# A fused stack of four cross-attention layers: norm weights loaded first, first clears and masks moved to other engines, and the low part of a query taken before its bf16 copy

## Chip, cores and metric

One core of a Trainium2 chip. The metric is the device time in microseconds, the median of several executions. Engines are called by their names: TensorE (PE), VectorE (DVE), ScalarE (ACT), GpSimd (POOL) and SyncE (SP), which issues most of the DMAs.

## The reference

Four cross-attention layers run one after the other on x (4 batches, 1024 tokens, 256 channels) with one context (154 keys of 512 values for each batch). Layers 0 and 2 are "wide": 16 heads of 64, with a suppression of four chosen keys by two token masks. Layers 1 and 3 are "narrow": an RMS norm of x, then 16 query heads of 16 on 4 key heads. All is float32.

```python
# wide layer
logits = einsum('bhqd,bhkd->bhqk', x @ Wq, ctx @ Wk) * 64 ** -0.5
logits[..., token_indices_A] += -20 * (1 - mask_A)      # and B
out = softmax(logits) @ (ctx @ Wv)
x = x + out @ Wo + bo
# narrow layer
xn = x * rsqrt(mean(x * x) + 1e-5) * norm_w
x = x + softmax(einsum(xn @ wq, ctx @ wk) / 4) @ (ctx @ wv) @ wo
```

## The kernel before

**Prepare (about the first 190 us).** `prepare` transposes the context and the tokens, and splits each of the 20 pieces of weights (10 for each pair of a wide and a narrow layer) into a high and a low part: SyncE loads a piece into one of four buffers (`load_piece`, L332), ScalarE copies it to a float32r high part (L420), GpSimd subtracts to get the low part (L448). TensorE makes keys and values from the pieces, VectorE takes the products out of PSUM (L295 to L311), SyncE stores them to DRAM (`store_job`, L198) from four output buffers. The piece "nq" (the narrow layer's query weights) is first multiplied by the norm weights, on ScalarE (L414). The norm weights have one small tile for both pairs, so the load for the second pair (L340) waits until ten high parts are made, and each load is issued right behind the piece nq.

**Layers.** A window is one batch of one pair, 8 windows in all. A window has 16 steps n of 4 heads each, 8 wide and 8 narrow; the order of all work is written out by hand in the strings FIRST, ORDER and LAST, and every engine walks through the same list and does its own share of each entry. Entries that matter here:

- "query n k": TensorE multiplies the tokens by the query weights into one of three PSUM banks (L1528). ScalarE copies it as the high part into `q_pair` (L1279, L1280). VectorE then does four instructions: two casts of the high part to bf16 into `q_aux` (L1438, L1439), after which it signals `dve_aux`, and two subtractions of the high part from the product in PSUM into `q_pair` (L1440, L1441), after which it signals `dve_query`. There are 160 such entries.
- "max n k": TensorE makes bf16 logits from `q_aux` and the bf16 keys (wide L1545, narrow L1549), into the next of the three banks; the first for a query waits for `dve_aux`. VectorE reduces them to a maximum for each row (L1451). There are 1024.
- "turn n": the maxima are transposed (L1558) and written back as rows of `q_aux` by ScalarE (L1304).
- "rest n", "score n k", "value n k": the exact logits (bf16 rows and low parts, L1587, plus float32r, L1588), the exponentials (ScalarE L1292), the products with the values.
- "scale", "norm", "low", "output": GpSimd multiplies by the inverse sums (L1402), ScalarE and VectorE split the result (L1341, L1464), TensorE multiplies by the output weights (L1649), VectorE adds to x (L1484).

A bank of the three is used in turn by query, max, turn, output, square, rate and give; TensorE waits before each use until the reader of the use three before is done, and the reader of a query's bank is `dve_query`.

**The start of the layers.** VectorE clears five tiles (L1427: `w_top`, the first half of `q_aux`, `w_aux`, `w_aux_rest`, `tops`); SyncE waits for them by count and loads keys, key rows (`load_top_rows`, L1002), mask rows (`load_masks`, L1109) and the rest. GpSimd makes the identity, clears the second half of `q_aux` and other tiles, waits for all of VectorE's clears, and fills rows.

```python
nc.vector.tensor_copy(q_aux[0:64, t, s, j, :], q_pair[0:64, s, j, :])                    # L1438
nc.vector.tensor_copy(q_aux[64:P, ...], q_pair[64:P, ...]).then_inc(dve_aux.sem, 1)      # L1439
nc.vector.tensor_tensor(q_pair[64:P, s, j, :], ps[0:64], q_pair[0:64, ...], ALU.subtract)
last = nc.vector.tensor_tensor(...)                                                      # L1441
last.then_inc(dve_query.sem, 1)
```

Of the kernel before, what the change touches and what calls it, by code (L numbers as in the profile page):

```python
# [22 lines left out]
P = 128  # L23
# [56 lines left out]
def prepare(nc, ins, dr):  # L80

    ctx = ExitStack()
    with ctx:  # L83
# [17 lines left out]
        normw = sb("p_normw", [P, KC])  # L101
# [229 lines left out]
        def _(sp):  # L331
            def load_piece(i):  # L332
                if i >= SETS:
                    sp.wait_ge(s_lo, i - SETS + 1)
                p, name, src, st = pieces[i]
                sp.dma_start(view(raw, i), src).then_inc(s_w[i % SETS], 16)
                if name == "nq":
                    if p:
                        sp.wait_ge(s_hi, len(pieces) // 2)
                    sp.dma_start(normw[:, :], ins[f"L{2 * p + 1}_xattn_norm_w"].rearrange("(k p) -> p k", p=P)).then_inc(s_nw, 16)  # L340

            with nc.allow_non_contiguous_dma(reason="columns of norm weights"):
# [11 lines left out]
                load_piece(1)  # L354
                for i in range(2, SETS):
                    load_piece(i)
# [49 lines left out]
        def _(act):  # L406

            for i, (p, name, src, st) in enumerate(pieces):
                act.wait_ge(s_w[i % SETS], 16 * (i // SETS + 1))
                wait_piece_free(act, i)  # L410
                if name == "nq":
                    act.wait_ge(s_nw, 16 * (p + 1))
                    for k in range(KC):
                        nc.scalar.activation(view(raw, i)[:, k], view(raw, i)[:, k], ACT.Copy,  # L414
                                             scale=normw[:, k:k + 1]).then_inc(s_evh, 1)
                    act.wait_ge(s_evh, KC * (p + 1))
# [451 lines left out]
def layers(nc, ins, dr, out):  # L868

    ctx = ExitStack()  # L870
    with ctx:
# [45 lines left out]
        ROWS_CLEARED, NARROW_ROWS_CLEARED, CLEARED = 5, 3, 10  # L917
# [8 lines left out]
        rows_cleared = sem("rows_cleared")  # L926
# [56 lines left out]

        def bank_of(use):
            return general[:, USE[use] % GB, :]
# [3 lines left out]
        def _(sp):  # L989
# [3 lines left out]

            def rows_of(buf, par):

                a = 64 * (1 - par)
                return buf[a:a + 6].rearrange("p (h two) k -> p h two k", two=2)[:, :, par, :]

            def load_top_rows(p):

                for par in range(2):
                    sp.dma_start(rows_of(w_top, par), dr["keyrows"][p][:, None, :].to_broadcast([6, 8, KEYS])).then_inc(top_rows_loaded, 16)  # L1002
# [101 lines left out]

            def load_masks(t):

                for par in range(2):
                    a = 64 * (1 - par)
                    sp.dma_start(q_aux[a:a + 6, t].rearrange("p s (j two) n -> p (s j) two n", two=2)[:, :, par, :],  # L1109
                                 dr["maskrows"][t][:, None, :].to_broadcast([6, 4, TOK])).then_inc(masks_loaded[t], 16)  # L1110
# [26 lines left out]
            def each_entry():  # L1137

                for w, what, c, k in PLAN:
# [84 lines left out]
                    elif what == "wkeys" and w > 0:  # L1224

                        if k == 0:
                            wait(sp, pe_value.sem, pe_value.after(w - 1, "value", 11, 1))
                            if w == B:
                                load_top_rows(1)
# [5 lines left out]
            load_top_rows(0)  # L1235
            sp.wait_ge(rows_cleared, 2)
            load_masks(0)
            sp.wait_ge(rows_cleared, 4)
# [4 lines left out]
            load_masks(1)  # L1243
# [10 lines left out]
        def _(act):  # L1254
            def do(it, what, n, k):
# [37 lines left out]
                elif what == "turn":  # L1293

                    if (it, n) == (0, 0):
                        act.wait_ge(rows_cleared, 2)
# [51 lines left out]
        def _(pool):  # L1348
            nc.gpsimd.memset(ident[:], 0.0).then_inc(ident_ready, 1)
# [75 lines left out]
        def _(dve):  # L1425
            for buf in (w_top[:], q_aux[:, 0], w_aux[:], w_aux_rest[:], tops[:]):
# [3 lines left out]
            def do(it, what, n, k):  # L1430
                if what == "query":
# [3 lines left out]
                    t, s, j = half_of(n), slot(n), 2 * k  # L1435
                    if (it, n, k) == (0, 8, 0):
                        dve.wait_ge(cleared, 1)
                    nc.vector.tensor_copy(q_aux[0:64, t, s, j, :], q_pair[0:64, s, j, :])  # L1438
                    nc.vector.tensor_copy(q_aux[64:P, t, s, j + 1, :], q_pair[64:P, s, j + 1, :]).then_inc(dve_aux.sem, 1)  # L1439
                    nc.vector.tensor_tensor(q_pair[64:P, s, j, :], ps[0:64], q_pair[0:64, s, j, :], ALU.subtract)  # L1440
                    last = nc.vector.tensor_tensor(q_pair[0:64, s, j + 1, :], ps[64:P], q_pair[64:P, s, j + 1, :], ALU.subtract)  # L1441
                    last.then_inc(dve_query.sem, 1)
                elif what == "max":
# [283 lines left out]
```

## Time and profile before

| | us |
|---|---|
| median of 3 runs | 1754.18 (1751.69 to 1755.21) |
| the profiled execution | 1748.67 |
| its span, first to last instruction | 1746.9 |
| TensorE matmuls busy | 1617.9 (93%) |
| TensorE weight loads busy | 882.6 (51%) |
| VectorE busy | 1197.9 (69%) |
| ScalarE busy | 1023.9 (59%) |
| GpSimd busy | 471.9 (27%) |

How to read the profile's rows: times are microseconds from the start of the span. A row of the timeline has the start, how long it took, the engine, the line, the operation, what was written from what, its shape, how many were merged, and in brackets how long the engine had been idle before it and whose end released it. SPq rows are DMA issues in SyncE's queue. A row of groups has the busy time and the mean in ns, then the idle time before them. Ends of matmuls are modelled, and spans on GpSimd are rough.

### The profile page before, as it was taken

The numbers are of one execution on the slowest core, as the hardware profiler recorded it, in microseconds if no ns is written. First come the engines' busy times: TensorE is split into PE (matmuls) and PEld (weight loads), VectorE is DVE, ScalarE is ACT, GpSimd is POOL, SyncE is SP. The second block draws the span as 40 slices with busy tenths as digits, with TensorE's granted clock in tenths as the row PEclk, the third lists the DMA queues.
The fourth block names the chain that finished last, engine by engine and source line by source line (L and its number), as shares of the span: only waits on it lengthen the run. The fifth ranks groups of instructions, "written<-read, shape, count | busy, mean of one in ns | idle before, by whom it ended". The sixth has DMA issues, their size and how long they took to land.

```text
span 1746.9 us, 29686 instructions
## 1 busy us (share of the span) xinstructions
PE 1617.9 (93%) x10732; PEld 882.6 (51%) x10732; DVE 1197.9 (69%) x2313; ACT 1023.9 (59%) x1737; POOL 471.9 (27%) x353
## 2 busy tenths in 40 slices
PE   7998698999999999999999999899999999999794
PEld 6886444444545454544545454445454545454442
DVE  5474547676777687768777777678777877775551
ACT  2111165666667676767666766576676767676452
POOL 5342402123222231223131313132322322232212
PEclk9898898999999999999999999999999999999986
DMA  7998402151315121512353323412151325131422
GB/s 255 323 317 242 140 25 58 37 98 28 84 32 132 27 78 27 131 35 80 69 115 91 73 54 80 91 40 72 41 122 27 82 41 125 26 81 23 123 69 81
DMA packets 176738, 160.57 MB, mean 92 GB/s; under 512 B 91722, under 2 KB 133066, under 8 KB 175570
## 3 DMA queue, kind: packets, MB, share of 16 engines
q1 hardware_dynamic: 174578, 150.29, 33.5%
q10 hardware_dynamic: 2016, 8.39, 1.2%
q8 instruction: 87, 1.43, 0.3%
q14 instruction: 57, 0.47, 0.1%
HBM read 115.11 MB, written 43.48 MB: 91 GB/s over the span
## 4 chain that ended last, share of the span: by engine, by line
PE 46%; issue 16%; DVE 10%; POOL 7%; ACT 3%; SPq 3%; DMA 3%; POOLq 0%; ACTq 0%; DVEq 0%
PE general L1649 9%; PE general L1528 7%; POOL kept L1402 4%; PE score_ps L1587 4%; PE score_ps L1588 4%; PE out_ps L1605 4%; PE general L1545 3%; PE general L1549 3%; PE score_ps L1576 2%; PE out_ps L1625 2%; DVE q_pair L1440 2%; DVE q_aux L1439 2%; SPq L1135 2%; DVE q_pair L1441 2%; PE general L1669 2%
## 5 line engine op out<-in xcount | busy, mean ns | idle before, releaser
L1451 DVE TENSOR_REDUCE tops<-general 128x2 bf16<-128x308 f32 x1024 | 433.2, 470 | 88.1 <-PE general L1545 40.1
L1292 ACT ACTIVATE probs<-score_ps 128x512 f32<-128x512 f32 x512 | 297.7, 598 | 141.0 <-PE score_ps L1588 128.0
L1402 POOL TENSOR_TENSOR kept<-kept,inv_b 128x512 f32<-128x512 f32 x128 | 170.7, 1355 | 464.9 <-DMA inv_b<-scratch_inverses 464.9
L1438 DVE CAST q_aux<-q_pair 64x512 bf16<-64x512 f32 x160 | 74.8, 468 | 194.1 <-ACT q_pair L1280 192.9
L1304 ACT ACTIVATE q_aux<-general 4x512 bf16<-4x512 bf16 x320 | 187.5, 586 | 31.7 <-PE general L1558 26.1
L1279 ACT ACTIVATE q_pair<-general 64x512 fp32r<-64x512 f32 x160 | 94.6, 591 | 156.7 <-PE general L1528 156.1
L1545 PE MATMUL general<-w_top,q_aux 128*128 128x154 bf16 x1024 | 133.4, 237 | 36.5 <-DVE q_pair L1441 26.1
L1341 ACT ACTIVATE a_hi<-kept 128x512 fp32r<-128x512 f32 x160 | 93.6, 624 | 112.0 <-POOL kept L1402 48.1
L1464 DVE TENSOR_TENSOR a_lo<-kept,a_hi 128x512 fp32r<-128x512 f32 x160 | 123.9, 807 | 49.7 <-ACT a_hi L1341 48.9
L1392 POOL TENSOR_TENSOR x_lo<-xn,x_hi 128x1024 fp32r<-128x1024 f32 x31 | 73.6, 2375 | 285.0 <-ACT x_hi L1260 145.6
L1588 PE MATMUL score_ps<-q_pair,w_pair 128*128 128x512 f32 x256 | 149.4, 589 | 0.0
L1588 PE MATMUL score_ps<-q_pair,n_pair 128*128 128x512 f32 x256 | 147.0, 586 | 0.0
L1484 DVE TENSOR_TENSOR x<-general,x 128x512 f32<-128x512 f32 x160 | 106.7, 689 | 57.3 <-PE general L1649 56.2
L1545 PEld LDWEIGHTS general<-w_top,q_aux 128*128 128x128 bf16 x1024 | 63.0, 98 | 161.1 <-issue 98.4
L1549 PE MATMUL general<-n_top,q_aux 128*128 128x308 bf16 x512 | 129.2, 306 | 13.4 <-DVE q_pair L1441 8.9
L1316 ACT ACTIVATE kept<-out_ps 128x512 f32<-128x512 f32 x192 | 104.3, 595 | 61.6 <-PE sum_ps L1619 47.7
L1605 PE MATMUL out_ps<-probs,w_val 128*64 128x512 f32 x512 | 135.7, 615 | 0.0
L1402 POOL TENSOR_TENSOR kept<-kept,inv_n 128x512 f32<-128x512 f32 x64 | 83.1, 1320 | 179.4 <-DMA inv_n<-scratch_inverses 179.4
L1649 PE MATMUL general<-a_hi,wo_hi 128*128 128x512 f32 x256 | 107.8, 421 | 9.1 <-DVE a_lo L1464 3.6
L1549 PEld LDWEIGHTS general<-n_top,q_aux 128*128 128x128 bf16 x512 | 40.7, 97 | 146.2 <-issue 66.7
L1528 PE MATMUL general<-x_hi,wq_hi 128*128 128x512 f32 x256 | 110.0, 430 | 4.1 <-PEq L83 3.6
L1440 DVE TENSOR_TENSOR q_pair<-general,q_pair 64x512 fp32r<-64x512 f32 x160 | 109.5, 684 | 5.0
(157 smaller groups left out, 3305.7 us busy)
## 6 DMA issues: line engine op xcount, KB each, us to landing
inv_b<-scratch_inverses SPq DMA_DIRECT2D x128, 256.0 KB, 4.8
w_pair<-scratch_wk_hi SPq DMA_DIRECT2D x32, 256.0 KB, 4.9
x<-scratch_stream SPq DMA_DIRECT2D x16, 512.0 KB, 3.3
inv_n<-scratch_inverses SPq DMA_DIRECT2D x256, 32.0 KB, 1.9
xn<-scratch_stream SPq DMA_DIRECT2D x15, 512.0 KB, 3.4
scratch_stream<-x SPq DMA_DIRECT2D x14, 512.0 KB, 4.9
scratch_wk_hi<-p_kout_hi SPq DMA_DIRECT2D x16, 308.0 KB
p_raw<-in_L_xattn_Wk_dram SPq DMA_DIRECT2D x4, 1024.0 KB, 7.8
```

Source lines behind the costliest of these rows:

```text
L1292: nc.scalar.activation(dst, score_ps[:, number % 2, :], ACT.Exp, scale=scale).then_inc(act_exp.sem, 1)
L1304: last = nc.scalar.activation(q_aux[a:a + 4, half_of(n), slot(n), j, :], ps[0:4].bitcast(BF16)[:, 0:TOK], ACT.Copy, scale=-1.0)
L1402: last = nc.gpsimd.tensor_tensor(tiles[i], tiles[i], (inv_b, inv_n)[n % 2][:, i, :], ALU.mult)
L1440: nc.vector.tensor_tensor(q_pair[64:P, s, j, :], ps[0:64], q_pair[0:64, s, j, :], ALU.subtract)
L1451: last = nc.vector.tensor_reduce(tops[:, n % 2, sub, 2 * pair:2 * pair + 2], src, AX_X, ALU.max)
L1464: last = nc.vector.tensor_tensor(a_lo[:, i, :], kept[:, place(tile), :], a_hi[:, i, :], ALU.subtract)
L1528: last = nc.tensor.matmul(ps, l, r, start=(i == 0), stop=(i == len(pairs) - 1))
L1545: last = nc.tensor.matmul(ps[:, i * KEYS:(i + 1) * KEYS], q[:, 2 * pair + i, sub], w_top[:, 4 * (n % 4) + 2 * pair + i, :], start=True, st ...
L1549: last = nc.tensor.matmul(ps[:, 0:2 * KEYS], q[:, n % 2, sub], n_top[:, h:h + 2, :].rearrange("p h k -> p (h k)"), start=True, stop=True)
L1588: last = nc.tensor.matmul(ps, keys[0], q_pair[:, s, unit, :], start=False, stop=True)
L1605: last = nc.tensor.matmul(out_ps[64 * i:64 * i + 64, k, :], w_val[:, h * DW:(h + 1) * DW], probs[:, 2 * k + i, :], start=True, stop=False, ...
L1649: last = nc.tensor.matmul(ps, l, r, start=(i == 0), stop=(i == len(pairs) - 1))
```

## The change

The norm weights get a tile with a column pair for each pair of layers; both loads are issued by SyncE between the second and the third piece, with no wait, and ScalarE waits for both. The clear of the first half of `q_aux` moves from VectorE to the head of GpSimd's list, with a semaphore of its own. The first load of the key rows and of the mask rows (four DMAs) is issued by ScalarE ahead of its first copy; SyncE's waits are adapted. In each query step VectorE does the two subtractions first and the two casts after them.

```diff
-        normw = sb("p_normw", [P, KC])
+        normw = sb("p_normw", [P, 2, KC])
...
-                if name == "nq":
-                    if p:
-                        sp.wait_ge(s_hi, len(pieces) // 2)
-                    sp.dma_start(normw[:, :], ins[f"L{2 * p + 1}_xattn_norm_w"].rearrange("(k p) -> p k", p=P)).then_inc(s_nw, 16)
...
                 load_piece(1)
+                for p in range(2):
+                    sp.dma_start(normw[:, p, :], ins[f"L{2 * p + 1}_xattn_norm_w"].rearrange("(k p) -> p k", p=P)).then_inc(s_nw, 16)
                 for i in range(2, SETS):
...
-                    act.wait_ge(s_nw, 16 * (p + 1))
+                    act.wait_ge(s_nw, 16 * 2)
...
-        ROWS_CLEARED, NARROW_ROWS_CLEARED, CLEARED = 5, 3, 10
+        ROWS_CLEARED, NARROW_ROWS_CLEARED, CLEARED = 4, 3, 10
...
             sp.wait_ge(rows_cleared, 1)
             load_wide_keys(0, 0, 0)
-            load_top_rows(0)
-            sp.wait_ge(rows_cleared, 2)
-            load_masks(0)
-            sp.wait_ge(rows_cleared, 4)
+            sp.wait_ge(rows_cleared, 3)
             load_aux_rows(0)
...
         @block.scalar
         def _(act):
+            act.wait_ge(rows_cleared, 1)
+            load_top_rows(act, 0)
+            act.wait_ge(first_cleared, 1)
+            load_masks(act, 0)
...
                     if (it, n) == (0, 0):
-                        act.wait_ge(rows_cleared, 2)
+                        act.wait_ge(first_cleared, 1)
...
         @block.gpsimd
         def _(pool):
+            nc.gpsimd.memset(q_aux[:, 0].bitcast(F32), 0.0).then_inc(first_cleared, 1)
             nc.gpsimd.memset(ident[:], 0.0).then_inc(ident_ready, 1)
...
-            for buf in (w_top[:], q_aux[:, 0], w_aux[:], w_aux_rest[:], tops[:]):
+            for buf in (w_top[:], w_aux[:], w_aux_rest[:], tops[:]):
...
+                    if (it, n, k) == (0, 0, 0):
+                        dve.wait_ge(first_cleared, 1)
                     if (it, n, k) == (0, 8, 0):
                         dve.wait_ge(cleared, 1)
-                    nc.vector.tensor_copy(q_aux[0:64, t, s, j, :], q_pair[0:64, s, j, :])
-                    nc.vector.tensor_copy(q_aux[64:P, t, s, j + 1, :], q_pair[64:P, s, j + 1, :]).then_inc(dve_aux.sem, 1)
                     nc.vector.tensor_tensor(q_pair[64:P, s, j, :], ps[0:64], q_pair[0:64, s, j, :], ALU.subtract)
                     last = nc.vector.tensor_tensor(q_pair[0:64, s, j + 1, :], ps[64:P], q_pair[64:P, s, j + 1, :], ALU.subtract)
                     last.then_inc(dve_query.sem, 1)
+                    nc.vector.tensor_copy(q_aux[0:64, t, s, j, :], q_pair[0:64, s, j, :])
+                    nc.vector.tensor_copy(q_aux[64:P, t, s, j + 1, :], q_pair[64:P, s, j + 1, :]).then_inc(dve_aux.sem, 1)
```

`load_top_rows` and `load_masks` take the issuing engine as an argument and are otherwise as before.

## Rows read from the trace of the kernel before

**Rows 1.** Stages: us, busy time of each engine, granted clock, DMA share, GB/s

```profile
400.00:1600.00 1200.00, 1159.89 (x8047) 590.08 (x8045) 901.85 (x1721) 809.50 (x1394) 320.96 (x225) 1.00 0.29 69
```

**Rows 2.** Waits of TensorE: us in total, times, longest

```profile
PE general L1545 <- DVE q_pair L1441: 26.1, 26, 3.4
...
PE general L1549 <- DVE q_pair L1441: 8.9, 9, 2.0
```

**Rows 3.** Timeline, the prepare stage, its start and its end

```profile
16.66 1.91 ACT L420 ACTIVATE p_hi<-p_raw 128x2048 fp32r<-128x2048 f32 x1 [0.86 <-DMA p_raw<-in_L_xattn_Wk_dram]
...
20.83 4.62 POOL L448 TENSOR_TENSOR p_lo<-p_raw,p_hi 128x2048 fp32r<-128x2048 f32 x1
...
152.38 0.46 SPq L340 DMA_DIRECT2D p_normw<-in_L_xattn_norm_w_dram  x1
...
157.10 2.85 SPq L215 DMA_DIRECT2D scratch_wv<-p_vout  x4
...
164.99 0.69 DVE L304 COPY p_vout<-p_ps 104x512 f32<-104x512 f32 x1 [6.31 <-DMA scratch_wv<-p_vout]
```

**Rows 4.** Timeline, the start of the layers

```profile
194.42 0.59 ACT L1279 ACTIVATE q_pair<-general 64x512 fp32r<-64x512 f32 x1 [29.41 <-PE general L1528]
...
194.52 1.76 DVE L1427 MEMSET q_aux<- 128x2048 f32 x1 [0.37 <-issue]
...
196.80 0.86 SPq L1002 DMA_DIRECT2D w_top<-scratch_keyrows  x2
...
197.71 0.65 SPq L1109 DMA_DIRECT2D q_aux<-scratch_maskrows  x2
...
198.21 0.42 DVE L1438 CAST q_aux<-q_pair 64x512 bf16<-64x512 f32 x1
...
200.23 0.41 PE L1545 MATMUL general<-w_top,q_aux 128*128 128x154 bf16 x2 [4.49 <-DMA q_aux<-scratch_maskrows]
```

**Rows 5.** Groups by line: busy us, mean ns | idle before, releasers

```profile
L1402 POOL TENSOR_TENSOR kept<-kept,inv_b 128x512 f32<-128x512 f32 x128 | 170.7, 1355 | 464.9 <-DMA inv_b<-scratch_inverses 464.9
...
L1441 DVE TENSOR_TENSOR q_pair<-general,q_pair 64x512 fp32r<-64x512 f32 x160 | 111.0, 693 | 2.2
...
L1439 DVE CAST q_aux<-q_pair 64x512 bf16<-64x512 f32 x160 | 90.2, 564 | 2.1
...
L1438 DVE CAST q_aux<-q_pair 64x512 bf16<-64x512 f32 x160 | 74.8, 468 | 194.1 <-ACT q_pair L1280 192.9
```

**Rows 6.** Timeline, query 8 of the first batch

```profile
258.13 0.42 DVE L1438 CAST q_aux<-q_pair 64x512 bf16<-64x512 f32 x1 [14.91 <-ACT q_pair L1280]
...
259.04 0.31 PE L1545 MATMUL general<-w_top,q_aux 128*128 128x154 bf16 x2 [2.18 <-DVE q_aux L1439]
```

**Rows 7.** Timeline, a query step that meets GpSimd's scaling

```profile
808.32 2.71 POOL L1402 TENSOR_TENSOR kept<-kept,inv_b 128x512 f32<-128x512 f32 x2 [5.50 <-DMA inv_b<-scratch_inverses]
808.43 1.45 DVE L1438 CAST q_aux<-q_pair 64x512 bf16<-64x512 f32 x1
...
812.88 0.30 PE L1545 MATMUL general<-w_top,q_aux 128*128 128x154 bf16 x2 [1.03 <-DVE q_pair L1441]
```

**Rows 8.** Timeline, a query step with GpSimd's scaling behind the casts

```profile
1240.33 0.42 DVE L1438 CAST q_aux<-q_pair 64x512 bf16<-64x512 f32 x1 [2.84 <-ACT q_pair L1280]
...
1240.92 2.65 POOL L1402 TENSOR_TENSOR kept<-kept,inv_n 128x512 f32<-128x512 f32 x2 [3.58 <-DMA inv_n<-scratch_inverses]
...
1243.38 0.57 PE L1549 MATMUL general<-n_top,q_aux 128*128 128x308 bf16 x3
```

**Rows 9.** Timeline, the first and the last of 48 query steps

```profile
267.88 0.42 DVE L1438 CAST q_aux<-q_pair 64x512 bf16<-64x512 f32 x1
...
269.17 2.49 POOL L1402 TENSOR_TENSOR kept<-kept,inv_b 128x512 f32<-128x512 f32 x2 [14.01 <-DMA inv_b<-scratch_inverses]
...
1588.60 0.42 DVE L1438 CAST q_aux<-q_pair 64x512 bf16<-64x512 f32 x1
...
1589.09 2.77 POOL L1402 TENSOR_TENSOR kept<-kept,inv_n 128x512 f32<-128x512 f32 x2 [18.28 <-DMA inv_n<-scratch_inverses]
```

More of the change, by code:

```diff
@@ L411, in _ @@
                 if name == "nq":
-                    act.wait_ge(s_nw, 16 * (p + 1))
+                    act.wait_ge(s_nw, 16 * 2)
                     for k in range(KC):
                         nc.scalar.activation(view(raw, i)[:, k], view(raw, i)[:, k], ACT.Copy,
-                                             scale=normw[:, k:k + 1]).then_inc(s_evh, 1)
+                                             scale=normw[:, p, k:k + 1]).then_inc(s_evh, 1)
                     act.wait_ge(s_evh, KC * (p + 1))
@@ L925, in layers @@
         cleared = sem("cleared")
-        rows_cleared = sem("rows_cleared")
+        rows_cleared, first_cleared = sem("rows_cleared"), sem("first_cleared")
         filled, rows_filled = sem("filled"), sem("rows_filled")
@@ L982, in last_query, with rows_of, load_top_rows, load_masks @@
             return (before_w, "query", 4 * before + 3, 1) if before % 2 == 0 else (before_w, "query", 4 * before + 2, 0)
+        def rows_of(buf, par):
+            a = 64 * (1 - par)
+            return buf[a:a + 6].rearrange("p (h two) k -> p h two k", two=2)[:, :, par, :]
+        def load_top_rows(eng, p):
+            for par in range(2):
+                eng.dma_start(rows_of(w_top, par), dr["keyrows"][p][:, None, :].to_broadcast([6, 8, KEYS])).then_inc(top_rows_loaded, 16)
+        def load_masks(eng, t):
+            for par in range(2):
+                a = 64 * (1 - par)
+                eng.dma_start(q_aux[a:a + 6, t].rearrange("p s (j two) n -> p (s j) two n", two=2)[:, :, par, :],
+                             dr["maskrows"][t][:, None, :].to_broadcast([6, 4, TOK])).then_inc(masks_loaded[t], 16)
         def bank_of(use):
@@ L992, in load_wide_query @@
                     sp.dma_start(wq[i][:, :, at:to].bitcast(F32), dr["wq_" + a][p, :, :, at:to]).then_inc(wide_query_loaded, 16)
[L994 to L1002, printed above, removed]
             def load_aux_rows(p):
@@ L1103, in load_early @@
                 sp.dma_start(xn[:], dr["stream"][bass.ds(b, 1), t].rearrange("o p k n -> p (o k) n")).then_inc(early_loaded.sem, 16)
[L1105 to L1110, printed above, removed]
             def store_x(c, w, b):
@@ L1228, in each_entry @@
                             if w == B:
-                                load_top_rows(1)
+                                load_top_rows(sp, 1)
                                 load_aux_rows(1)
@@ L1242, in _ @@
             sp.wait_ge(cleared, 1)
-            load_masks(1)
+            load_masks(sp, 1)
             load_x(0, 0)
```

## The prediction

> **What bounds the kernel now.** I read the stage table first, then TensorE's waits, then single stretches of the timeline. In the long middle TensorE is busy 1159.89 of 1200 us, VectorE 901.85, GpSimd 320.96 [rows 1]. So only TensorE's gaps can be won there, and a step on VectorE costs time only where TensorE waits for it. The reader should see in the waits that a gap of TensorE before a group of maxima is mostly a wait for a query's last subtraction (L1441): 26.1 us in 26 gaps before wide groups, 8.9 us in 9 before narrow ones [rows 2]. That is the wait for a PSUM bank: TensorE has three, and the query's is freed by the low part. The maxima wait on the other product of the same step, the bf16 copy. The edit swaps the two.
>
> **Part 1, norm weights.** The second load leaves SyncE's queue at 152.38 (0.46 us), and the wait on ten high parts goes with it. SyncE then stores products from 157.10, and VectorE stood 6.31 us at 164.99 for such a store to land [rows 3]; what leaves the queue ahead of it counts: -0.5 us. The first load leaves SyncE's queue in the same way a hundred microseconds earlier; that is in the far end only. Both loads are now issued near the start, 2 x 0.46 us ahead of the third weight piece. ScalarE copied that piece at 16.66 to 18.57, and GpSimd took it up only at 20.83 [rows 3]: 2.3 us of cover over 0.9, so nothing. If the cover is gone, +0.9. Ends for the part: -1.5 and +0.9.
>
> **Part 2, the first clears and masks.** VectorE loses the 1.76 us clear of the query rows, which stands between its first clear and its first query at 198.21 [rows 4]. It would be free near 196.3. But ScalarE now issues four DMAs first; on SyncE these four took 0.86 and 0.65 us [rows 4]. ScalarE started its first copy at 194.42; after the first clear (over by 194.5) and 1.5 us of issues it starts at 195.7, and its two copies of 0.59 us put VectorE's first query at about 196.9: 1.3 us earlier, not 1.9. SyncE's later loads move up 1.5 us, which nobody waits for. The masks that TensorE waited for until 200.23 [rows 4] were issued at 197.71 and are now issued by 195.7, so the casts end last; their coming second costs nothing here, since VectorE works through both queries before its first maximum. GpSimd's other clears start up to 1.76 us later; it then waited for VectorE's last clear anyway, and its row fills are needed only a whole query later: nothing, or +0.4 if uncovered. Take -1.3; ends -1.9 (the whole clear) and +1.5 (ScalarE's issues fully in the way). The constant offsets into the two-column weight tile change nothing.
>
> **Part 3, subtractions first, 160 times.** Two casts have means 468 and 564 ns, a subtraction 693 [rows 5]. So a bank comes free at least 0.84 us sooner, the bf16 copies 1.4 us later, and the total is the same. Three effects.
>
> (a) The sooner bank. The bound is 35.0 us [rows 2]. Most of it does not come: VectorE begins its next maximum only after all four instructions, as now, and TensorE can be three banks ahead at most, so its gap reappears two groups later. What counts is a gap after which TensorE has other work, as at 812.88 (1.03 us) [rows 7]. I take a fifth, 7 us; ends 0 and -20.
>
> (b) The later copy. The group that reads it usually comes after the whole query step is over; the gap row for that wait shows once, at 259.04: VectorE casts at 258.13 and TensorE starts 0.05 us after the second cast, after 2.18 us of idleness [rows 6]. It now waits two subtractions longer, 1.4 us, and behind it on TensorE stands the next query, for which VectorE waits. I add 0.5 us for other places where the reader follows closely: +1.9, ends +1 and +4.
>
> (c) Collisions with GpSimd. The casts last 165.0 us in all [rows 5]; a pair undisturbed takes 0.84, as at 1240.33 [rows 8] and 267.88 [rows 9], 134.9 for 160. The 30.1 left over fall on a few steps where GpSimd multiplies: at 808.43 one cast took 1.45 us, under a GpSimd pair at 808.32 to 811.03 [rows 7]. The subtractions never stretch; reading PSUM, they pass beside GpSimd. Now look at where GpSimd begins: at 1240.92, 0.6 us after the query step, when both casts were out of the way [rows 8]. In the new order the first cast would begin at 1241.7, in the middle of GpSimd's 2.65 us; it waits out the first multiplication (to 1242.2), the second cast waits out the second (to 1243.6) and ends at 1244.0, 3.7 us after the step's start instead of 0.84. I went through all 160 steps, letting a cast that finds GpSimd busy wait until that instruction ends: in the old order this gives 30.2 us (the trace 30.1), with the casts 1.38 us later 58, in 48 steps (the first and last stand in [rows 9]) instead of 25. An independent bound agrees: GpSimd is busy 0.267 of the time [rows 1], a multiplication lasts 1.355 us [rows 5], so 320 casts at random would wait 320 x 0.267 x 0.68 = 58 us. Moving the start by up to 0.6 us either way leaves 55 to 58. So VectorE gets about 28 us more. TensorE feels it where a run of maxima comes next: at 1243.38 [rows 8] it stands 3.05 us behind the step's start, and the copy would now be ready at 3.7. Where an output or a low part follows, VectorE has idle time. I take 45%, +12.6; ends 0 and +28.
>
> The Trainium skill (State Buffer, Who interferes with whom) says that a cast in a two-port mode and a GpSimd instruction exclude each other for a whole instruction, whichever began first. By that rule GpSimd loses as well, up to 0.42 us in each of 23 added steps, which would make the sum up to 10 us larger; GpSimd, however, idles 464.9 us waiting for wide inverses [rows 5], so I add nothing. The trace agrees as far as the cast goes, 1.45 us against 0.42.
>
> **Sum.** -0.5 -1.3 -7 +1.9 +12.6 = +5.7 us. The profiled execution took 1748.67 us (span 1746.9 and 1.8 around it), 5.5 below the median of 1754.18; I put the same difference on the median: 1760. A measurement of this kernel can tell about 0.2% (3.5 us) from no change.
>
> **Rivals.**
> Release wins (faster). The sooner bank decides, and the collisions stay on VectorE, which is idle a quarter of the middle. For: 35 us of gaps name L1441. Against: gaps before maxima come back two groups later. It needs TensorE to feel under a fifth of (c): -0.5 -1.3 -7 +1.9 and nothing for (c) is -7, 1747; with a third of the bank gaps, 1743. Chance 0.22.
> Balance. TensorE feels a quarter of the collisions, +7: the sum is 0, 1754. Chance 0.16.
> Collisions in full. Every late cast becomes late TensorE: -0.5 -1.3 -7 +1.9 +28 = +21, 1775. For: the three banks leave no room in a run of maxima. Against: about a third of the 48 steps are followed by an output, a low part or another query. Chance 0.10.
> The start does not gain, as ScalarE's issues delay its first copies by all they save VectorE: the sum without -1.3 is +7, 1761. Chance 0.04.
> The forecast, the sum above with (c) between 8 and 17, has 0.48.
>
> **Range and chances.** The forecast's own range is 1755 to 1766: (c) at 8 gives +1, at 17 gives +10, and the smaller ends of parts 1 and 2 add 1 to 2 on top. For 8 in 10 it reaches down to the first rival's 1747, with 2 us more for its bank gaps, and halfway up to the full collisions: 1745 to 1770, which leaves out most of the full collisions and the far end of (a). Faster is the first rival and a sliver of the balance, 0.24. Within 0.2% is the rest of the balance and the foot of the forecast, 0.18. Slower is the remaining forecast with the full collisions and the start that does not gain, 0.58.
>
> **What would show it.** In the changed kernel's groups, the two casts together should last about 190 us instead of 165.0, the subtractions the same. The waits on L1441 should nearly vanish, and waits on the casts' line should take their place before maxima. VectorE's first query should start near 197, ScalarE's first copy near 195.7, and the group after query 8 of the first batch 1.4 us further from its query. The prepare stage should end 0.5 us sooner. The forecast is wrong if the casts' total stays near 165 (the multiplications have moved along with the queries), or if it rises and TensorE's gaps in the middle still shrink below their 40 us.

## The result, and the profile after

The changed kernel takes 1760.76 us (median of 10 runs, 1756.55 to 1764.45); the kernel before, run beside it, takes 1749.88 (10 runs, 1744.47 to 1756.1). The ratio is 1.0064, with a 95% interval of 1.0048 to 1.0081: slower, by some 11 us. The forecast was 1760.0 against a median of 1754.18, +5.7 us; the time was met better than the difference, because the three runs had put the kernel before 4.3 us too high. That part of the hit is luck. The profiled execution took 1762.38 us with a span of 1760.2.

A "batch" from here on is one of the eight windows, counted from 0, and a "chunk" is one of its steps of four heads. The edits move the lines of the layers by two or three: the subtractions are L1441 and L1442, the copies (the "casts" of the forecast) L1444 and L1445, the wide and narrow groups of maxima L1548 and L1552.

The stage table of the changed kernel, for the stretch of [rows 1]; the columns are the busy time of each engine with its instructions in brackets, TensorE's granted clock, the DMA share and GB/s:

```profile
400.00:1600.00 1200.00, 1150.23 (x7939) 585.54 (x7940) 912.64 (x1703) 800.31 (x1378) 316.90 (x221) 0.99 0.29 69
```

TensorE is busy 9.7 us less of the same 1200 than in [rows 1], VectorE 10.8 us more. TensorE's gaps grew from 40.1 to 49.8 us. The groups by line (busy us, mean ns, then the engine's idle time before them) say what VectorE does longer:

```profile
L1442 DVE TENSOR_TENSOR q_pair<-general,q_pair 64x512 fp32r<-64x512 f32 x160 | 111.0, 694 | 2.2
...
L1445 DVE CAST q_aux<-q_pair 64x512 bf16<-64x512 f32 x160 | 101.5, 634 | 2.1
L1444 DVE CAST q_aux<-q_pair 64x512 bf16<-64x512 f32 x160 | 92.1, 576 | 5.0
...
L1403 POOL TENSOR_TENSOR kept<-kept,inv_b 128x512 f32<-128x512 f32 x128 | 170.7, 1354 | 464.3 <-DMA inv_b<-scratch_inverses 464.3
```

The copies take 193.6 us together, 28.6 more than in [rows 5]; the subtractions of the query step and GpSimd's multiplications take what they took. The waits of TensorE (us in total, times, longest) against [rows 2]:

```profile
PE general L1552 <- DVE tops L1454: 19.0, 19, 2.4
...
PE general L1548 <- DVE q_aux L1445: 10.3, 4, 3.6
...
PE general L1548 <- DVE xn L1498: 6.0, 14, 0.5
PE general L1548 <- DVE q_pair L1442: 5.0, 3, 3.0
```

The 26.1 us in front of wide groups that waited for a subtraction are 5.0; those in front of narrow groups have left the head of the list. In their place stand waits for the copies (10.3 us in 4) and for VectorE's later work, maxima and the residual's product (19.0, 6.0, and 7.2 us for maxima before wide groups). That these rows replaced the old ones is what the edit was bound to do. What it cost stands in the idle time of TensorE before these groups, from the groups by line: before wide groups it is the same, 36.5 and then 35.7 us, before narrow groups it doubled, from 13.4 to 26.3 us.

One step in close-up. Query 12 of batch 5 is the step of [rows 8], which the forecast had worked through. The timeline (start, duration, engine, line, in square brackets the idle time before) of the changed kernel:

```profile
1249.06 0.68 DVE L1441 TENSOR_TENSOR q_pair<-general,q_pair 64x512 fp32r<-64x512 f32 x1 [2.85 <-ACT q_pair L1280]
...
1249.51 2.69 POOL L1403 TENSOR_TENSOR kept<-kept,inv_n 128x512 f32<-128x512 f32 x2 [3.44 <-DMA inv_n<-scratch_inverses]
...
1250.48 0.58 DVE L1444 CAST q_aux<-q_pair 64x512 bf16<-64x512 f32 x1
1251.08 1.41 DVE L1445 CAST q_aux<-q_pair 64x512 bf16<-64x512 f32 x1
...
1252.55 0.56 PE L1552 MATMUL general<-n_top,q_aux 128*128 128x308 bf16 x3 [0.36 <-DVE q_aux L1445]
```

Both copies stand behind GpSimd's two multiplications, and the step ends 3.43 us after it began, where 3.7 had been worked out. VectorE loses 1.15 us here and TensorE stands idle for 0.36: it had other work until 0.36 before. That ratio, not the collision, is the uncertain part of the whole case.

Query 8 of batch 0, the step of [rows 6], and the start of the layers against [rows 4]:

```profile
193.19 0.76 PE L1531 MATMUL general<-x_hi,wq_hi 128*128 128x512 f32 x1 [3.62 <-PEq L83]
...
194.60 1.13 ACTq L990 DMA_DIRECT2D w_top<-scratch_keyrows  x2
...
195.77 0.70 ACTq L996 DMA_DIRECT2D q_aux<-scratch_maskrows  x2
...
196.52 0.59 ACT L1279 ACTIVATE q_pair<-general 64x512 fp32r<-64x512 f32 x1 [31.55 <-DVE tops L1428]
...
197.80 0.68 DVE L1441 TENSOR_TENSOR q_pair<-general,q_pair 64x512 fp32r<-64x512 f32 x1 [1.35 <-issue]
...
200.56 0.44 PE L1548 MATMUL general<-w_top,q_aux 128*128 128x154 bf16 x4 [1.91 <-DVE q_aux L1445]
...
261.14 0.44 PE L1548 MATMUL general<-w_top,q_aux 128*128 128x154 bf16 x2 [3.60 <-DVE q_aux L1445]
```

VectorE's first query comes 0.41 us sooner than in [rows 4], 4.61 us after TensorE's first query matrix product against 5.44 (198.21 less 192.77, where TensorE starts in the profile before). The two profiles differ in TensorE's clock here: from 193 to 197 us the granted clock is 1.00 in the kernel before and 0.50 in the changed one (2.4 and 1.2 GHz), and one of these first products takes 0.39 and 0.63 us. Other kernels with the old order show low clocks at this point too (0.65 and 0.50), so it is not the new order, and single profiles can't be compared closely here. The gap before the group of query 8 is 3.60 us instead of 2.18. And the prepare stage, against [rows 3]:

```profile
4.50 1.89 SPq L352 DMA_DIRECT2D p_normw<-in_L_xattn_norm_w_dram  x2
...
155.83 2.85 SPq L215 DMA_DIRECT2D scratch_wv<-p_vout  x4
...
165.03 0.69 DVE L304 COPY p_vout<-p_ps 104x512 f32<-104x512 f32 x1 [7.00 <-DMA scratch_wv<-p_vout]
```

The stores leave 1.27 us sooner and land no sooner.

**Where along the span it is lost.** One matrix product of TensorE (the first eight of the scores for a wide chunk) marks the same point of the plan in both kernels: chunk 3 of batch 0, chunk 1 of batch 2 and chunk 1 of batch 6. First the kernel before, then the changed one:

```profile
247.21 1.07 PE L1576 MATMUL score_ps<-q_pair,w_rest 128*32 128x512 f32 x8
...
572.92 1.07 PE L1576 MATMUL score_ps<-q_pair,w_rest 128*32 128x512 f32 x8
...
1307.25 1.06 PE L1576 MATMUL score_ps<-q_pair,w_rest 128*32 128x512 f32 x8
```

```profile
247.88 1.06 PE L1579 MATMUL score_ps<-q_pair,w_rest 128*32 128x512 f32 x8
...
578.33 1.06 PE L1579 MATMUL score_ps<-q_pair,w_rest 128*32 128x512 f32 x8
...
1316.09 1.06 PE L1579 MATMUL score_ps<-q_pair,w_rest 128*32 128x512 f32 x8
```

To the first mark the changed kernel is 0.67 us behind. Between the first two marks it takes 330.45 instead of 325.71 us (+4.7), in the four middle batches between the second and the third 737.76 instead of 734.33 (+3.4), and from there to the end of the span 444.11 instead of 439.65 (+4.5). The traces of the experiments below show how far these can be trusted. The middle stretch takes 732.86 to 734.33 us in the three with the copies first there and nothing else changed in it, 737.76 and 737.88 in the two with the subtractions first everywhere: the +3 to +5 us are real. The last stretch is 445.14 us in the kernel with parts 1 and 2 alone, which has the old order: the +4.5 us there are no more than what single executions differ by.

### The profile page after: what moved, and what is told of

Read it like the earlier page. It is cut to its first block, busy times and chain, and to the rows that moved or that the text cites. A ratio compares the mean times of both kernels' runs of the same rounds, so it can differ in the third digit from the quotient of the medians.

```text
span 1760.2 us, 29686 instructions
## 1 busy us (share of the span) xinstructions
PE 1624.9 (92%) x10732; PEld 886.7 (50%) x10732; DVE 1220.3 (69%) x2312; ACT 1024.1 (58%) x1737; POOL 475.3 (27%) x354
## 4 chain that ended last, share of the span: by engine, by line
PE 44%; issue 14%; DVE 13%; POOL 7%; ACT 4%; SPq 4%; DMA 3%; POOLq 0%; ACTq 0%; DVEq 0%
PE general L1652 9%; PE general L1531 8%; PE score_ps L1591 4%; PE score_ps L1590 4%; POOL kept L1403 4%; PE out_ps L1608 3%; PE general L1548 3%; PE general L1552 3%; DVE q_aux L1445 2%; DVE q_aux L1444 2%; DVE q_pair L1442 2%; DVE q_pair L1441 2%; PE score_ps L1579 2%; PE out_ps L1628 2%; SPq L1133 2%
## 5 line engine op out<-in xcount | busy, mean ns | idle before, releaser
L1403 POOL TENSOR_TENSOR kept<-kept,inv_b 128x512 f32<-128x512 f32 x128 | 170.7, 1354 | 464.3 <-DMA inv_b<-scratch_inverses 464.3
L1441 DVE TENSOR_TENSOR q_pair<-general,q_pair 64x512 fp32r<-64x512 f32 x160 | 109.5, 684 | 205.5 <-ACT q_pair L1280 202.8
L1548 PE MATMUL general<-w_top,q_aux 128*128 128x154 bf16 x1024 | 136.5, 237 | 35.7 <-DVE q_aux L1445 10.3
L1552 PE MATMUL general<-n_top,q_aux 128*128 128x308 bf16 x512 | 129.6, 307 | 26.3 <-DVE tops L1454 19.0
L1467 DVE TENSOR_TENSOR a_lo<-kept,a_hi 128x512 fp32r<-128x512 f32 x160 | 118.7, 774 | 42.8 <-ACT a_hi L1341 41.8
L1548 PEld LDWEIGHTS general<-w_top,q_aux 128*128 128x128 bf16 x1024 | 62.7, 98 | 163.4 <-issue 75.6
L1552 PEld LDWEIGHTS general<-n_top,q_aux 128*128 128x128 bf16 x512 | 40.7, 98 | 158.7 <-DVE tops L1454 67.3
L1442 DVE TENSOR_TENSOR q_pair<-general,q_pair 64x512 fp32r<-64x512 f32 x160 | 111.0, 694 | 2.2
```

The costliest lines, as they stand in the source:

```text
L1403: last = nc.gpsimd.tensor_tensor(tiles[i], tiles[i], (inv_b, inv_n)[n % 2][:, i, :], ALU.mult)
L1548: last = nc.tensor.matmul(ps[:, i * KEYS:(i + 1) * KEYS], q[:, 2 * pair + i, sub], w_top[:, 4 * (n % 4) + 2 * pair + i, :], start=True, st ...
L1552: last = nc.tensor.matmul(ps[:, 0:2 * KEYS], q[:, n % 2, sub], n_top[:, h:h + 2, :].rearrange("p h k -> p (h k)"), start=True, stop=True)
```

## The experiments

Ten kernels were measured, each beside the kernel before on the same chip; an amount in us is the ratio times the kernel before unless medians are named. The theory: the loss is the order in the query step, and in it the copies that now meet GpSimd. The rivals: it is the start of the kernel (parts 1 and 2), or the copies being late whoever else works.

**Which part of the change it is.** First the order alone, on the kernel before:

```diff
-                    nc.vector.tensor_copy(q_aux[0:64, t, s, j, :], ...)
-                    nc.vector.tensor_copy(q_aux[64:P, t, s, j + 1, :], ...).then_inc(dve_aux.sem, 1)
                     nc.vector.tensor_tensor(q_pair[64:P, s, j, :], ..., ALU.subtract)
                     last = nc.vector.tensor_tensor(q_pair[0:64, s, j + 1, :], ..., ALU.subtract)
                     last.then_inc(dve_query.sem, 1)
+                    nc.vector.tensor_copy(q_aux[0:64, t, s, j, :], ...)
+                    nc.vector.tensor_copy(q_aux[64:P, t, s, j + 1, :], ...).then_inc(dve_aux.sem, 1)
```

> The kernel before with the two subtractions of a query put first, and nothing else of the change. Collision theory (the copies, now later, meet GpSimd's multiplications): nearly the whole loss is here, +10 to +14 us against the kernel before, and VectorE's copies take about 193 us in all instead of 165.0. Start theory (the loss comes from the loads and clears at the start): 0 to +3 us.

Measured: 1758.85 us against 1750.19, ratio 1.0055 (1.0034 to 1.0076), +9.6 us (6.0 to 13.3), just under the 10 to 14 expected. Its groups of copies:

```profile
L1442 DVE CAST q_aux<-q_pair 64x512 bf16<-64x512 f32 x160 | 102.3, 639 | 2.1
L1441 DVE CAST q_aux<-q_pair 64x512 bf16<-64x512 f32 x160 | 89.8, 561 | 5.0
```

192.1 us together, as expected. Then the other two parts, with the copies put first again in the changed kernel (the diff above, turned round):

> The changed kernel with the two copies put first again: norm weights, clears and masks alone. Collision theory: -1 to +1 us against the kernel before, with the stage of products beginning some 0.4 us later and no gain of the first query left by the end of the first group. Start theory: +8 to +11 us.

Measured: 1750.54 us, ratio 0.9996 (0.9977 to 1.0016). The start is worth nothing either way, within 4 us; the order carries the loss.

**Is it the meeting with GpSimd?** The multiplications are cut to 8 of 512 columns, in both orders (the other columns stay unscaled):

```diff
-                        last = nc.gpsimd.tensor_tensor(tiles[i], tiles[i], (inv_b, inv_n)[n % 2][:, i, :], ALU.mult)
+                        last = nc.gpsimd.tensor_tensor(tiles[i][:, 0:8], tiles[i][:, 0:8], (inv_b, inv_n)[n % 2][:, i, 0:8], ALU.mult)
```

> The kernel before, with GpSimd's two multiplications of a scaling step cut to 8 of 512 columns (the other columns stay unscaled, so that part of the normalisation is left out). Copies first. Collision theory: a base for the next kernel; the two copies together take 138 to 142 us instead of 165.0 (the subtractions of the splits are still there to meet), and the time is 5 to 15 us under the kernel before. Release theory (only the PSUM bank counts): copies as said, the time within 5 us of the kernel before.

> The kernel before with GpSimd's multiplications cut to 8 of 512 columns (the same part of the normalisation left out), and the subtractions first. Collision theory: without the multiplications the new order costs little, so this kernel is between 5 us faster and 3 us slower than the same cut with the copies first. Late-copy theory (TensorE waits for the copies whoever else works): 8 to 12 us slower than the same cut with the copies first, as in the whole kernel.

Measured: copies first 1708.56 us (ratio 0.9757, 0.973 to 0.9783), subtractions first 1713.16 (0.9792, 0.9764 to 0.9819). The first expectation was far too small, 42 us instead of 5 to 15; more on that below. Between the two orders lie 4.6 us by the medians, 6 by the ratios, whose intervals overlap. That is between the two expectations (at most 3, and 8 to 12) and decides for neither: as far as time tells, about half of the 9.6 us is still there without the multiplications. TensorE's idle time before the groups of maxima says the same. The new order adds 13 us to it in the kernel with all multiplications (47.7 in the kernel with parts 1 and 2 alone, 60.6 with the order alone) and 6.6 without them (33.7 and 40.3). The groups of copies, copies first and then subtractions first:

```profile
L1439 DVE CAST q_aux<-q_pair 64x512 bf16<-64x512 f32 x160 | 69.4, 434 | 2.1
L1438 DVE CAST q_aux<-q_pair 64x512 bf16<-64x512 f32 x160 | 68.6, 429 | 212.3 <-ACT q_pair L1280 211.3
```

```profile
L1441 DVE CAST q_aux<-q_pair 64x512 bf16<-64x512 f32 x160 | 76.0, 475 | 5.0
L1442 DVE CAST q_aux<-q_pair 64x512 bf16<-64x512 f32 x160 | 70.5, 441 | 2.1
```

138.0 and 146.5 us: the new order adds 8.5 us instead of 27.1. In the trace they are copies that meet what was left in on GpSimd. Three of them meet a subtraction of a split (L1392, the low part of the tokens of a wide or narrow layer) and take 2.35 us each, which is 5.8 us; most of the rest meet the additions behind the narrow multiplications (L1406). These two profiles are the slowest execution of the one kernel (1711.93) and the fastest of the other (1710.36), so they are compared by stretches and not by their ends. The same three marks, copies first and then subtractions first:

```profile
249.78 1.07 PE L1576 MATMUL score_ps<-q_pair,w_rest 128*32 128x512 f32 x8
...
566.80 1.07 PE L1576 MATMUL score_ps<-q_pair,w_rest 128*32 128x512 f32 x8
...
1284.84 1.06 PE L1576 MATMUL score_ps<-q_pair,w_rest 128*32 128x512 f32 x8
```

```profile
244.38 1.06 PE L1576 MATMUL score_ps<-q_pair,w_rest 128*32 128x512 f32 x8
...
566.36 1.06 PE L1576 MATMUL score_ps<-q_pair,w_rest 128*32 128x512 f32 x8
...
1283.00 1.06 PE L1576 MATMUL score_ps<-q_pair,w_rest 128*32 128x512 f32 x8
```

Between the first two marks the new order costs 5.0 us (321.98 against 317.02) also without the multiplications. Part of that may be a lead given back. To the first mark the kernel with the subtractions first is 3.1 us ahead, counted from TensorE's first query product (193.46 and 191.20), in a stretch where its granted clock was 0.90 against 0.82. Counted from there to the second mark the new order costs 1.8 us. In the middle batches it costs nothing: 716.64 against 718.04, 1.4 us less. From there to the ends of the spans (1710.1 and 1708.5) it is +0.2. So the loss of the middle batches needs the multiplications (+3 to +5 us with them, -1.4 without), and 1.8 to 5 us of the loss of the first two batches does not. For the last batches nothing is shown.

These two traces also show what became of the sooner bank. In batch 4, at the same point, copies first and then subtractions first:

```profile
940.54 0.30 PE L1545 MATMUL general<-w_top,q_aux 128*128 128x154 bf16 x2 [0.77 <-DVE q_pair L1441]
...
942.48 2.93 DVE L1451 TENSOR_REDUCE tops<-general 128x2 bf16<-128x308 f32 x7
...
945.30 0.50 PE L1528 MATMUL general<-x_hi,nq_hi 128*128 128x512 f32 x1
```

```profile
938.26 0.30 PE L1545 MATMUL general<-w_top,q_aux 128*128 128x154 bf16 x2
...
940.38 0.69 PE L1545 MATMUL general<-w_top,q_aux 128*128 128x154 bf16 x4 [0.37 <-DVE xn L1495]
...
941.08 2.93 DVE L1451 TENSOR_REDUCE tops<-general 128x2 bf16<-128x308 f32 x7
...
943.90 0.50 PE L1528 MATMUL general<-x_hi,nq_hi 128*128 128x512 f32 x1
```

With the subtractions first, TensorE has no gap before the group; it starts it 2.82 us ahead of VectorE's run of seven maxima (941.08 less 938.26) instead of 1.94. The run of maxima itself begins where VectorE is done with the whole step, so TensorE stands 0.37 us at the third bank, and further on again. Its next query product begins 1.40 us sooner than in the other kernel (943.90 and 945.30), and so did VectorE's run of maxima (941.08 and 942.48): the 0.9 us that the sooner bank put on top are lent and given back within 6 us.

**The late copy by itself.** The subtractions first in two steps only. The diff shows the line that chooses, here and in the next two kernels; "low" puts the two subtractions first and "copies" the two copies:

```diff
...
+                    order = "low" if (it, n, k) in ((0, 8, 0), (0, 12, 0)) else "copies"
...
```

> The kernel before, with the subtractions first in only two of the 160 query steps: queries 8 and 12 (first half) of the first batch, after which TensorE waited for the copies in every kernel with the low part first. Late-copy theory: the row of TensorE's first group after query 8 is 1.4 to 2.8 us later, that after query 12 another 1.4, and the whole is 2.5 to 3.5 us slower, with VectorE's copies still near 165 us in all. Collision theory in its pure form (all of the loss comes with the longer copies): no change, within 1 us.

Measured: 1753.63 us, ratio 1.0015 (0.9996 to 1.0033), +2.6 us. TensorE's gap before the group of query 8, and its scores for chunks 3 and 8 of batch 0:

```profile
249.38 1.06 PE L1580 MATMUL score_ps<-q_pair,w_rest 128*32 128x512 f32 x8
...
262.63 0.31 PE L1549 MATMUL general<-w_top,q_aux 128*128 128x154 bf16 x2 [3.60 <-DVE q_aux L1442]
...
283.78 1.22 PE L1580 MATMUL score_ps<-q_pair,w_rest 128*32 128x512 f32 x8
```

The gap is 3.60 instead of 2.18 us, and the stretch between the two scores 34.40 us instead of 32.57 (279.78 less 247.21 in the kernel before): 1.8 us for query 8, by one trace of each; the traces with the old order spread over 31.82 to 32.57 us here. Query 12 added nothing: the expectation of another 1.4 us there was a misreading, as the wait behind it belongs to query 14, whose copies met a split's subtraction. The copies take 171.4 us in all, not the 165 expected; 3.44 of them are one copy at 210.96, ahead of the two steps that were changed.

**The middle batches alone.**

```diff
+                    order = "low" if 2 <= it <= 6 else "copies"
...
```

> The kernel before, with the subtractions first in batches 2 to 6 only (the even middle). VectorE's copies should take 180 to 185 us in all instead of 165.0 either way. If TensorE feels 45% of that, as forecast: 7 to 9 us slower. If the middle absorbs it and the loss sits in the first and last batches, as the shift between the two traces suggests: 1 to 4 us slower.

Measured: 1755.83 us, ratio 1.0027 (1.0009 to 1.0044), +4.7 us with an interval of 1.6 to 7.7; the copies take 187.3 us, somewhat more than the 180 to 185 expected. The time lies between the two expectations, and its interval reaches into both. Five of the eight batches give about half of the order's loss; the copies there carry 22.3 of the 27.1 us, and TensorE felt about a fifth of those (7 to 35% by the interval).

**Each step in the order that misses GpSimd.**

```diff
+                    order = "low" if 1 <= it <= 6 and (n, k) in ((8, 1), (10, 0), (14, 0)) else "copies"
...
```

> The kernel before, with the subtractions first only for queries 8 (second half), 10 (first half) and 14 of batches 1 to 6: the steps whose copies met GpSimd in the old order and mostly did not in the new one. If the collisions are the price of an order: VectorE's copies fall from 165.0 to 148 to 155 us and the time by 2 to 6 us. If they only move to other steps: copies above 160 us and no change, within 2 us.

Measured: 1742.56 us, ratio 0.9944 (0.9922 to 0.9966), faster than the kernel before by 8 us by the medians (1750.49) and 10 by the ratio, where 2 to 6 had been expected. The copies:

```profile
L1442 DVE CAST q_aux<-q_pair 64x512 bf16<-64x512 f32 x160 | 77.6, 485 | 2.1
L1441 DVE CAST q_aux<-q_pair 64x512 bf16<-64x512 f32 x160 | 76.3, 477 | 184.3 <-ACT q_pair L1280 182.7
```

153.9 us, 11.1 less than before. The same edit that costs 10 us over all steps brings 8 where it takes copies out of GpSimd's way. This is the strongest evidence for the theory: here the new order makes the copies shorter, and the sign of the time follows them. The middle stretch of its trace takes 727.11 us, 7.2 less than in the kernel before. The rival, that the sooner bank of these steps does it, would have to bring more than it brought in all steps without the multiplications (1.4 us in that stretch).

**Starting the whole step sooner.** VectorE idles 192.9 us, by the profile before, for ScalarE's second copy of a query, though half of its work needs only the first:

```diff
-                    nc.scalar.activation(q_pair[0:64, s, j, :], ps[0:64], ACT.Copy)
+                    nc.scalar.activation(q_pair[0:64, s, j, :], ps[0:64], ACT.Copy).then_inc(act_half.sem, 1)
...
-                    wait(dve, act_query.sem, act_query.after(it, what, n, k))
+                    wait(dve, act_half.sem, act_half.after(it, what, n, k))
...
                     nc.vector.tensor_copy(q_aux[0:64, t, s, j, :], ...)
                     nc.vector.tensor_tensor(q_pair[64:P, s, j, :], ps[0:64], ..., ALU.subtract)
+                    wait(dve, act_query.sem, act_query.after(it, what, n, k))
                     nc.vector.tensor_copy(q_aux[64:P, t, s, j + 1, :], ...).then_inc(dve_aux.sem, 1)
                     last = nc.vector.tensor_tensor(q_pair[0:64, s, j + 1, :], ps[64:P], ..., ALU.subtract)
```

> The kernel before, with VectorE started after the first of ScalarE's two copies of a query: it makes the first half's bf16 copy and subtraction, then waits for ScalarE's second copy and does the other half. The copies stay ahead of the subtractions, half by half. VectorE waits 192.9 us in 113 places for these two ScalarE copies, so each step can end up to 0.59 us sooner. Release theory (what counts is when bank and copy are ready): 4 to 15 us faster. Rival (the gap comes back two groups later, as it did for the sooner bank): within 2 us.

Measured: 1724.05 us, ratio 0.9837 (0.9815 to 0.986), 26 us under the kernel before by the medians and more than either theory gave. The first of its waits on the subtraction, and the step of [rows 8] once more:

```profile
PE general L1547 <- DVE q_pair L1443: 10.6, 15, 2.8
```

```profile
1221.36 0.42 DVE L1439 CAST q_aux<-q_pair 64x512 bf16<-64x512 f32 x1 [2.24 <-ACT q_pair L1280]
...
1222.49 0.42 DVE L1442 CAST q_aux<-q_pair 64x512 bf16<-64x512 f32 x1
1222.55 2.73 POOL L1403 TENSOR_TENSOR kept<-kept,inv_n 128x512 f32<-128x512 f32 x2 [3.58 <-DMA inv_n<-scratch_inverses]
```

The waits on the subtraction fell from 26.1 and 8.9 us [rows 2] to 10.6 and 1.7, and the others hardly rose (low parts 10.0 instead of 7.9 us). TensorE's idle time before all groups of maxima fell from 49.9 to 23.8 us, as much as the whole gain: bank, copies and VectorE's next maxima all come sooner, by up to one ScalarE copy, 0.6 us. The second copy here slips in 0.06 us ahead of GpSimd. The copies take 158.5 us in all, 6.5 less than before, so most of the gain is not from collisions.

Two variants of it. The subtraction ahead of the copy in each half:

```diff
-                    nc.vector.tensor_copy(q_aux[0:64, ...], ...)
                     nc.vector.tensor_tensor(q_pair[64:P, s, j, :], ..., ALU.subtract)
+                    nc.vector.tensor_copy(q_aux[0:64, ...], ...)
                     wait(dve, act_query.sem, ...)
```

> The kernel that lets VectorE start after ScalarE's first copy of a query, now with the subtraction ahead of the bf16 copy in each half (copies 0.69 us later than in that kernel, not 1.38). That kernel ran at 0.9837 of the kernel before, with 158.5 us of copies. Collision theory: the later copies meet GpSimd more often again, 165 to 185 us of copies, and the time is 3 to 10 us above that kernel. Rival (with VectorE's step ending sooner the order has stopped to matter): within 2 us of that kernel.

Measured: 1730.07 us (0.9868, 0.9838 to 0.9898), copies 166.1 us. By the medians it is 6.0 us behind the version with the copies first, as the collision theory had it, though the two intervals overlap, so this is a hint only. And that version with both subtractions ahead of both copies in the steps that still met GpSimd:

```diff
+                    if 1 <= it <= 6 and (n, k) in ((8, 1), (14, 0)):
+                        ...
+                    else:
```

> The kernel that lets VectorE start after ScalarE's first copy, with both subtractions first only for query 8 (second half) and query 14 of batches 1 to 6, whose copies still met GpSimd there (3.2 us and 2.6 to 3.3 us for steps that take 2.2 us undisturbed). If both gains add up: copies below 153 us instead of 158.5 and 1 to 5 us faster than that kernel, 27 to 32 us under the kernel before. If the collisions only move: the same as that kernel within 1 us.

Measured: 1727.38 us (0.9855, 0.9829 to 0.988), 22 us under the kernel before by the medians, copies 159.0 us: no gain, and the copies did not get shorter in sum, which is the expectation that collisions only move. A list of steps chosen by hand fits one timing of the kernel and not the next; the gain of the previous list was not carried over.

## Why the forecast was right, and where its terms were not

The direction, the range and the place (the order in the query step) were right. The order was forecast at +7.5 us (-7 +1.9 +12.6) and measured at +9.6 (interval 6.0 to 13.3) by itself. That the two are so near is luck: in the sum two errors of about 5 us cancelled.

(c) Collisions. The size on VectorE was right: 28 us forecast, 27.1 with the order alone, 28.6 in the changed kernel, and 193.6 us of copies against about 190. The close-up of query 12 came out at 3.43 instead of 3.7 us. The share that TensorE feels was put at 45%. With the order alone the loss less the 1.8 us of the late copy is 7.8 of 27.1 us, 29%; in batches 2 to 6 it was about a fifth, and in the kernel with chosen steps 7.9 us of time, by the medians, for 11.1 us of copies, 70%. It is no constant. The close-ups suggest that it depends on whether TensorE has other work behind the step; no run varied that. The term was sized too high, some 8 us instead of 12.6 (4 to 12 by the interval, with (a) near nothing). Not all of it is the multiplications that the forecast had named: without them the order still cost 4.6 to 6 us, with intervals that overlap. That the term exists and has this sign is what the chosen steps and the middle stretch with and without the multiplications show.

(a) The sooner bank. Forecast -7, and this is the step that failed most: "I take a fifth, 7 us". The argument just before it (VectorE begins its next maximum only after all four instructions, so the gap reappears two groups later) is what the rows of batch 4 show: the gap comes back. Without multiplications the middle batches gain 1.4 us in four. The term was about -1 to -2 us, an estimate from that one pair of traces. The kernel that starts the step at half is the counterpart: there the end of VectorE's step moves, and the waits fall for good.

(b) The later copy. The place was right, the gap went from 2.18 to 3.60 us, exactly the 1.4 worked out. It cost 1.8 us by the trace where 1.4 plus 0.5 for other places had been taken: right in sum. With the order alone the same stretch takes 34.47 us, in the changed kernel 35.37. The last 0.9 us go with a granted clock of 0.77 instead of 0.81, at which TensorE was busy 25.06 us instead of 23.94 with the same products.

Not foreseen as a term of its own: the copies also meet the subtractions of the splits. Between the first two marks the new order costs 5.0 us without multiplications; up to 1.8 of it is (b), and in the trace the rest sits at query 14 of batch 0 and query 6 of batch 1, whose copies ran into a split. The sweep through all 160 steps had counted them within (c).

Part 1, norm weights. Forecast -0.5. SyncE did store sooner (155.83 instead of 157.10), but VectorE then waited 7.00 us instead of 6.31 for the store to land, and went on at 165.03 instead of 164.99. The queue was not what the store waited for. The two issues at the start took 1.89 us, not 2 x 0.46, and ScalarE's copy of the third piece came at 17.41 instead of 16.66. What that does to the end can't be read: kernels with the same prepare stage begin the layers anywhere from 191.20 to 196.43 us (the cut multiplications with subtractions first, and the chosen steps). A term of 0.5 us there is below what single profiles can hold.

Part 2, clears and masks. Forecast -1.3; VectorE's first query was to start near 196.9 and ScalarE's first copy near 195.7. They started at 197.80 and 196.52. The four issues took 1.83 us on ScalarE instead of 1.5, and the first had to wait for VectorE's first clear, over at 194.56. Counted from TensorE's own start, VectorE gained 0.83 us, and the first group of maxima 0.09 (200.56 less 193.19 against 200.23 less 192.77): with the masks no longer last, the copies are, and they now stand behind the subtractions. That is the rival "the start does not gain", which had 0.04; it was true alongside the forecast, not instead of it. The kernel with parts 1 and 2 alone, at 0.9996, agrees with a sum of zero, and its interval (-4 to +3 us) with the -1.8 forecast as well; only the rows speak against a gain.

"Release wins" fell with (a), and "collisions in full" with the share. "Balance", with a quarter of the collisions felt, had the share of (c) nearly right; it failed because the -7 of (a) did not come.

## What to carry to other kernels

When instructions are reordered within one engine's step, ask first whether the end of the step moves: a buffer freed sooner inside it only lent time here, where its next user again waited for the same engine. Then lay the moved instructions against what other engines do in those microseconds; an order that is free by itself can put a short instruction behind a long one of a neighbour. And when an engine idles for the second of two parts, start it on the first: a finer semaphore was worth nearly three times what the order was.

## What the runs showed that had not been expected

Cutting GpSimd's multiplications to 8 columns brought 42 us, where 5 to 15 had been expected from the copies alone. The low part of the output shows one more source; the kernel before, then the one with small multiplications and copies first:

```profile
L1464 DVE TENSOR_TENSOR a_lo<-kept,a_hi 128x512 fp32r<-128x512 f32 x160 | 123.9, 807 | 49.7 <-ACT a_hi L1341 48.9
```

```profile
L1464 DVE TENSOR_TENSOR a_lo<-kept,a_hi 128x512 fp32r<-128x512 f32 x160 | 105.9, 696 | 25.7 <-ACT a_hi L1341 24.5
```

In the kernel before, the low parts take 123.9 us, 807 ns each, and up to 1783 ns; here 105.9 and 696. Both of their inputs lie in SBUF. So subtractions do get longer beside GpSimd. Those of the query step, with one input in PSUM, take 684 and 693 ns in both kernels, and none of the 160 at L1441 more than 695: "the subtractions never stretch" held for them alone. Copies and low parts together give back 27.0 + 18.0 = 45 us of VectorE. How much of the 42 us is that, and how much the scaled tiles being ready a microsecond sooner each time, was not separated.

The Trainium skill (SBUF — State Buffer, Who interferes with whom) says that the shared pair of ports is locked for a whole instruction by whichever comes first, and that a VectorE instruction with two SBUF inputs takes part as well as one in a two-port mode, when GpSimd's reads SBUF. The rows agree for VectorE's side, for both kinds: copies up to 1.45 us against 0.42, low parts up to 1783 ns against 696. That GpSimd would lose as much when VectorE is first does not show in its rows: its wide multiplications average 1355 ns in [rows 5], 1354 in the changed kernel, and the narrow pair of the step above lasts 2.69 us against 2.65, so nothing was to be added for it, as forecast. GpSimd's spans are rough, and no run here isolates it.
